# Stores of the convolved image begun by GpSimd in a queue of its own, instead of by SyncE

## The reference

```python
def _gn(v, G=32, eps=1e-5):              # normalised per image over groups of 8 channels
    ...
x = x + conv3x3_depthwise(sign(_gn(x)), sign(kernel))            # layer 0
x = x + gated_block(_gn(x), ...)                                 # layer 1

def gated_block(x, ...):
    ca_gate = sigmoid(fc(mean(x, (1, 2))) + fc(max(x, (1, 2))))  # per image and channel
    xc = x * ca_gate
    m = mean(xc, channels); y = state_space_scan(m)              # over the 12544 pixels of an image
    s = conv7x7([mean(xc, channels), max(xc, channels)])
    x2 = xc * sigmoid(y) + xc * sigmoid(s)
    return relu(batchnorm(x2))                                   # statistics over the whole batch
```

## Time and profile before

| | |
|---|---|
| runs | 3921.43, 3962.74, 3990.44 us; median 3962.74 us |
| profiled execution | 3909.51 us, span 3907.8 us |
| granted TensorE clock in it | 0.815 of full speed |
| DMA moved | 1226.37 MB, mean 314 GB/s |
| first block | 0 to about 2150 us of the span |

### The profile page before, as it was taken

One profiled execution on the slowest core, in us unless ns is written; L12 is line 12 of the kernel. 1 busy time (PEld: TensorE's weight loads), 2 busy tenths in 40 slices (PEclk: granted clock), 3 DMA queues, 4 the chain that ended last, 5 costly groups with the idle time before them and its releaser, 6 DMA issues. The chain is left out here.

```text
span 3907.8 us, 50951 instructions
## 1 busy us (share of the span) xinstructions
PE 2742.0 (70%) x16873; PEld 1716.9 (44%) x16873; DVE 3318.0 (85%) x4658; ACT 2857.3 (73%) x4087; POOL 13.6 (0%) x14
## 2 busy tenths in 40 slices
PE   5787779777877887788777694333337767777776
PEld 3454455445544554454453321000005555555555
DVE  4898889888988898889889546998889999999997
ACT  3676687668767876787777345887778888888887
POOL 1000000000000000000000000000000000000000
PEclk9999899889989998998888886555557887777777
DMA  3887787779777877797767355999958999999998
GB/s 133 304 302 268 284 331 288 271 292 340 275 270 294 337 272 268 295 343 265 280 257 258 83 126 191 413 413 389 389 234 356 426 428 428 424 420 422 421 423 344
DMA packets 249518, 1226.37 MB, mean 314 GB/s; under 512 B 33419, under 2 KB 36219, under 8 KB 234982
## 3 DMA queue, kind: packets, MB, share of 16 engines
q1 hardware_dynamic: 249318, 1223.79, 81.0%
HBM read 805.14 MB, written 418.57 MB: 313 GB/s over the span
## 5 line engine op out<-in xcount | busy, mean ns | idle before, releaser
L884 PE MATMUL psum<-signs,taps 128*128 128x448 bf16 x4032 | 893.1, 372 | 194.4 <-DVE signs L616 187.6
L1478 PE MATMUL psum<-ident,xt 128*128 128x128 f32 x3136 | 562.1, 349 | 274.8 <-ACT stage L1512 223.0
L1478 PEld LDWEIGHTS psum<-ident,xt 128*128 128x128 f32 x3136 | 500.1, 212 | 363.3 <-ACT stage L1512 303.6
L884 PEld LDWEIGHTS psum<-signs,taps 128*128 128x128 bf16 x4032 | 401.4, 102 | 567.4 <-DVE signs L616 194.7
L421 ACT ACTIVATE xt<-psum 128x896 f32<-128x896 f32 x448 | 407.0, 910 | 248.3 <-PE psum L796 239.4
L1287 PE MATMUL psum<-signs,ones 3*128 3x448 bf16 x896 | 329.3, 511 | 366.9 <-DMA signs<-gate_scratch 225.1
L796 PE MATMUL psum<-ident,stage 128*128 128x128 f32 x3136 | 464.3, 298 | 151.4 <-DMA stage<-x_dram 75.3
L1512 ACT ACTIVATE stage<-psum 128x512 f32<-128x512 f32 x784 | 406.5, 614 | 170.0 <-DMA out_dram<-stage 149.2
L1533 DVE SCALAR_TENSOR_TENSOR xc<-xt,curs,psum 128x1792 f32<-128x1792 f32 x224 | 456.1, 2077 | 81.0 <-PE psum L1287 77.0
L796 PEld LDWEIGHTS psum<-ident,stage 128*128 128x128 f32 x3136 | 402.3, 155 | 208.7 <-DMA stage<-x_dram 86.2
L1348 ACT ACTIVATE xc<-xc 128x1792 f32<-128x1792 f32 x224 | 380.0, 1697 | 127.1 <-DVE xc L1369 127.1
(11 more groups left out here) (152 smaller groups left out, 2348.4 us busy)
## 6 DMA issues: line engine op xcount, KB each, us to landing
xt<-x_scratch SPq DMA_DIRECT2D x210, 1792.0 KB
stage<-x_dram SPq DMA_DIRECT2D x224, 896.0 KB, 7.2
x_scratch<-xt SPq DMA_DIRECT2D x224, 896.0 KB, 5.2
out_dram<-stage SPq DMA_DIRECT2D x112, 1792.0 KB, 13.6
xc<-x_scratch SPq DMA_DIRECT2D x210, 896.0 KB, 9.0
xc<-ssm_scratch SPq DMA_DIRECT2D x24, 512.0 KB, 5.0
signs<-gate_scratch SPq DMA_DIRECT2D x217, 10.5 KB
feat_scratch<-hsum SPq DMA_DIRECT2D x112, 7.0 KB
```

The source lines that it names most:

```text
L884: ins = nc.tensor.matmul(turn[h % 2][:, b * 512:b * 512 + HB], taps[:, j, t, :], moving, start=t == 0, stop=t == 8)
L1478: last = nc.tensor.transpose(out_ps[k % 4][:, v * C + j * P:v * C + (j + 1) * P], block_in, ident[:, :])
```

## The change

The wait and the DMA of `store` leave SyncE's list and become a loop on GpSimd, in the same order over images, units and halves. The bytes, the addresses, the semaphore waited for (`added`) and the one raised (`stored[u][j]`) stay. All other engines have the same instructions as before.

```diff
@@ sync: image(i)
-                def store(i, u, j):
-                    sp.wait_ge(added, i * NTILE + 4 * u + 2 * j + 2)
-                    sp.dma_start(x1_d[i, j, :, :].rearrange("c (a n) -> c a n", a=2)[:, :, u * TP:(u + 1) * TP],
-                                 unit(j, u)).then_inc(stored[u][j], 16)
...
                     for h in range(NP):
-                        if h >= 1:
-                            store(i, (h - 1) // 2, (h - 1) % 2)
                         if h >= 4 and more:
                             load_next_x(i + 1, h - 1)
...
                     if more:
                         load_next_x(i + 1, NP - 1)
-                    store(i, NU - 1, NJ - 1)
                     if channels:
                         load_next_g(i - 1, NP - 1)
@@ gpsimd: behind the constants
+                for i in range(NB):
+                    for u in range(NU):
+                        for j in range(NJ):
+                            pool.wait_ge(added, i * NTILE + 4 * u + 2 * j + 2)
+                            pool.dma_start(x1_d[i, j, :, :].rearrange("c (a n) -> c a n", a=2)[:, :, u * TP:(u + 1) * TP],
+                                           unit(j, u)).then_inc(stored[u][j], 16)
```

## The result

The changed kernel took 3987.68 us in the median of 6 runs (3969.49 to 4006.83), the kernel before 3976.59 us in its 6 (3896.54 to 4003.81): +0.3% by the medians.

The account below looks back on a forecast made before the run. VectorE was taken to bound a step and x(13)'s landing an image's end. 43.5 us gained in 15 tails and 11 us lost on VectorE gave -32.5 us, -0.8%: 3930 us, range 3865 to 4050.

Parts of the forecast that it names:

- The bound: First block: VectorE bounds a step, and the landing of input piece x(13) sets the end of an image.
- The price of 15 us for 1 us of landing: Image tails: moving the landing of x(13) by 1 us moves the time 15 times, 15 us or 0.38%.
- The head start at x(9): Input load x(9), no longer behind a store waiting for VectorE, would be issued about 3 us earlier.
- x(12)'s wait: Tail: TensorE's wait of 1.75 us for input piece x(12) would go, since it would land well before 1352.
- The line ahead of x(13): Transfers queued before x(13): earlier loads shorten the queue, so x(13) lands 2.8 to 5.0 us earlier; 2.9 taken.
- the queue can run nearly dry before x(12): DMA queue late in an image: little is carried over, making x(13) the fourth or fifth transfer from 1343.8.
- The last store was priced: End of an image: the last store, in its own queue, takes up to one transfer, 2.2 us, from x(13).
- The forecast for a tail: Each of 15 tails: x(13) lands 2.9 us earlier and the tail shortens by as much, 43.5 us in sum.
- 11 us: VectorE beside GpSimd's work: 0.05 us lost for each of 224 stores, bounds 0 and 242 us.
- rival C: Steps: GpSimd beginning stores holds VectorE up; +46 us at 0.4 us each, up to +242; chance over 2%: 0.20.
- Rival B: Tail: the last store overtakes, earlier loads bring nothing, x(13) lands 2.2 us later; +33 us, +0.8%; chance 0.22.
- In a queue of its own it lands earlier: Tail: the last unit's store, already 2.6 us ahead of the copy needing it, would land earlier from GpSimd's queue.

Follow-up runs that it names:

- the version with 7.4: First block alone of the kernel before, with g loads 11 and 12 issued behind x(13) instead of ahead of it: 2152.60 us against 2205.55.
- the changed block: First block of the changed kernel alone, all stores on GpSimd and the other three blocks left out: 2218.18 us against 2205.55 before.

## Why the prediction was wrong

- **The bound was read rightly.** A step is VectorE's, and the landing of x(13) sets the tail: the table above is in one order by landing and by time. The price of 15 us for 1 us of landing was rough. Going from 12.35 to 11.0 us gave 30 us, from 11.0 to 7.4 only 23, and in the version with 7.4 the copies wait for a store instead.
- **The head start at x(9) came as predicted** (x(9) goes 2.85 us ahead of the store of its step, forecast about 3), and x(12)'s wait went.
- **The step that failed** is "The line ahead of x(13)", in the words "the queue can run nearly dry before x(12)", which made x(13) the fourth or fifth transfer from 1343.8. It didn't run dry. In the profile before, four transfers were outstanding when x(12) was issued at 1342.86 (they landed at 1343.8, 1346.0, 1349.4 and 1351.6). In the changed one, at 1348.66, there were four again: x(11) (landed at 1349.6), the store of 1342.61 (1353.1), the g load of 1342.21 (1354.8) and the store of 1348.66 (1357.5). A head start of 3 us at x(9) is no head start at x(13): x(13)'s issue didn't move, my own numbers had it at 0.4 us for x(12), and by my own sum a step brought 6.6 us of work in 6.1 us, so a line grows there and doesn't drain.
- **What that term measured.** Without the last store x(13) was to be the fourth, 5.0 us sooner (1358.1 - 1353.1). The run with the last store on SyncE measures this term: 1.35 us sooner (12.35 to 11.0). With the last store on GpSimd in both, the other 13 give 1.6 us (14.5 to 12.9).
- **The last store was priced rightly** at 2.2 us, the distance between fourth and fifth: it costs 2.2 us without the head start (12.35 to 14.5) and 1.9 with it (11.0 to 12.9). The forecast for a tail was -5.0 + 2.2, near the -2.9 that I wrote (the numbers give 2.8); measured are -1.35 to -1.6 and +1.9 to +2.2, in sum +0.57 us.
- **Not costed at all**: TensorE's clock behind the tail. The first 18 matmuls of an image take 0.2 to 0.4 us longer in the three pairs of traces, and the first `pack` comes at least 0.3 us later, about 5 us in 15 tails, most of the rest of the 12.6 us. That the waits, now joined into one, keep the clock down is argued, not shown. The run's mean clock isn't the measure of it: in the version with only the last store on GpSimd it is 0.903, as low as in the changed block (0.904), and the first `pack` comes 13.96 us after L585, no later than before (14.12).
- **VectorE** lost about 0.1 us an image, 1.5 us in all, where I had put 11 us and rival C up to 242 us. GpSimd's instruction takes 0.69 us and the stores were in time: from the second image on no copy waited for one.
- **Rival B was the outcome** in its mechanism. Its sum of +33 us is too large for the change, since it gave the head start nothing, and its sign (14 us or more for x(13)) didn't come: 12.9. With the last store alone on GpSimd both came, 14.5 us and +28 us. I had put against it that the store of 1324.08 took only 5.0 us, "so nothing was in front of it". That was misread: the g load issued at 1317.55 was still outstanding, until 1326.5, and 4.0 us is the shortest that any store took.
- **"In a queue of its own it lands earlier"** holds for the last store only (9.3 us against 11.7). The median of all stores went from 5.2 to 8.8 us. It is 9.5 us with SyncE's loads ahead of its stores, so this is the order too, and not GpSimd.
- **The measure.** The whole kernel's spread comes in the main from the fourth block's DMA rate, 422 or 364 GB/s in profiles of the same code, which is 80 to 100 us. I read the spread of 1.7% as a plain uncertainty and took the frame of the median for it. My range (3865 to 4050) holds the measured 3987.68 us, but it is 185 us wide; the sign is wrong.

The rule of the Trainium skill in "DMA: Bandwidth & Descriptors", section "Issuing engines are not separate DMA queues" (all queues run on the same 16 engines and interleave), agrees with the traces, and the interleaving is the very thing that costs: with one queue x(13) and the last store landed in the order of issue, 2.2 us apart, and with two the store passed x(13) in 10 images of 15. The rule of the Trainium skill in "SBUF — State Buffer", section "SBUF: two separate sides" (a GpSimd operation and an instruction of VectorE in one of its modes with two ports, which a float32 copy within SBUF brings about, block each other), agrees with the one such copy here, L702, which takes 0.265 us instead of 0.170 with GpSimd's store beside it. But it costs 0.1 us, less than the 0.29 us that GpSimd's row goes on behind the copy's start. L597 keeps 0.68 us beside GpSimd's DMA instruction; whether it uses two ports no run shows.

## What to carry to other kernels

Follow one late transfer back through its queue, and count what is issued ahead of it in bytes: here 2.2 us for each 896 KB, and moving two loads that were hardly needed yet (one wait of 1.9 us) gained four times what moving the stores cost. A head start is worth only what is left of it where the line ends. The second queue added no rate here (279 GB/s in the first block against 280), it took away an order, so before splitting one ask which transfer was meant to be last. If whole runs spread by more than the effect, cut the kernel down to the block that was changed.

## What the runs showed of the hardware

- A store begun by GpSimd goes in fewer, larger packets. The pages, section 3 (queue, packets, MB, share), first before, then the two queues of the changed kernel:

```profile
q1 hardware_dynamic: 249318, 1223.79, 81.0%
q1 hardware_dynamic: 188390, 1018.25, 68.2%
q0 software_dynamic: 32256, 205.54, 12.5%
```

  That is 32256 / 224 = 144 packets a store, where SyncE's queue lost (249318 - 188390) / 224 = 272. The shortest landing of a store is 4.0 us in both.
- SyncE issues an input load in 0.61 us (median) directly behind a store and in 0.33 us otherwise: before, 150 of 224 loads follow a store, in the changed kernel none.
- GpSimd starts its DMA instruction 0.3 us after the end of the VectorE instruction that releases it (1322.35 to 1322.64), where SyncE takes 0.03 us, and is busy for 0.69 us (0.68 to 0.80).
- While it is, a float32 copy of 128 x 4 on VectorE takes 0.265 us instead of 0.170; the longer instructions L597, L616 and L712 keep their times within 0.003 us.
- The fourth block moves 420 to 426 GB/s at first (2950 to 3200 us). In four of the five profiles of whole kernels it falls to 363 or 364 GB/s, between 3200 and 3400 us, also in kernels without a DMA from GpSimd. Why stays open.
